# Expert routing taken one attention step earlier, and two shared gating products ahead of the last group's slots

## What is computed

```python
scores = jax.nn.softmax(x2d @ wg_router.T, axis=-1)
topk_w, topk_idx = jax.lax.top_k(scores, TOP_K)
topk_w = topk_w / (jnp.sum(topk_w, axis=-1, keepdims=True) + 1e-20)
pos = jnp.cumsum(oh, axis=0) - 1            
valid = pos_in_e < C
xe = jnp.zeros((E, C, D), x2d.dtype).at[flat_idx, safe_pos].add(x_rep)
...
sh = jax.nn.silu(x2d @ ws_gate) * (x2d @ ws_up) @ ws_down
return y + sh
```

## Time and profile before

| | us |
|---|---|
| median of 3 runs | 635.13 (633.89 to 639.38) |
| the profiled execution's own time | 637.68 |
| its span, first to last instruction | 635.8 |
| DVE busy | 493.5 (78%) |
| PE busy, matmuls | 489.2 (77%) |
| ACT busy | 336.2 (53%) |
| POOL busy | 216.5 (34%) |

### The profile page before, as it was taken

One profiled execution on the slowest core, in us unless ns is written; L12 is line 12 of the kernel. 1 busy time (PEld: TensorE's weight loads), 2 busy tenths in 40 slices (PEclk: granted clock), 3 DMA queues, 4 the chain that ended last, 5 costly groups with the idle time before them and its releaser, 6 DMA issues.

```text
span 635.8 us, 13234 instructions
## 1 busy us (share of the span) xinstructions
PE 489.2 (77%) x4916; PEld 402.2 (63%) x4916; DVE 493.5 (78%) x963; ACT 336.2 (53%) x663; POOL 216.5 (34%) x165
## 2 busy tenths in 40 slices
PE   0268889897725598898959659989999999999930
PEld 0147667675514376676746435589999999999930
DVE  2997999999475789999963680379999999999910
ACT  4334565655565155657532521257777777777720
POOL 3000000000000000000007277508888888888881
PEclk9977999999957699999968988999999999999985
DMA  8999910000000000000002173375997869779323
GB/s 296 282 240 234 249 34 3 1 2 2 2 2 0 0 2 1 3 3 2 1 2 104 31 276 113 125 258 161 244 232 195 227 173 247 203 192 253 37 27 66
DMA packets 56720, 71.89 MB, mean 113 GB/s; under 512 B 11777, under 2 KB 45036, under 8 KB 56544
## 3 DMA queue, kind: packets, MB, share of 16 engines
q1 hardware_dynamic: 40272, 57.35, 31.2%
q0 software_dynamic: 16400, 13.87, 11.0%
HBM read 42.09 MB, written 37.04 MB: 124 GB/s over the span
## 4 chain that ended last, share of the span: by engine, by line
DVE 51%; PE 28%; issue 12%; ACT 5%; DMA 2%; POOL 1%; DVEq 1%; POOLq 0%; SPq 0%; ACTq 0%
DVE negmax L1219 9%; PE S L751 4%; DVE both L1087 3%; DVE wgu_s L1477 3%; DVE fwd L1075 3%; PE S L782 3%; DVE xgT L1496 3%; PE PJ L701 3%; DVE sg L1505 3%; PE S L769 3%; PE S L940 3%; DVE ek L1502 3%; DVE hidden_s L1511 3%; DVE wgu_s L1479 2%; PE S L786 2%
## 5 line engine op out<-in xcount | busy, mean ns | idle before, releaser
L999 PE MATMUL S<-xgT,wgu_s 128*128 128x384 f32 x576 | 108.0, 340 | 8.2 <-DVE sg L1505 7.4
L374 POOL DMA_INDIRECT xe_rows<-x_tok,slot_i x48 | 47.7, 994 | 177.6 <-issue 165.8
L999 PEld LDWEIGHTS S<-xgT,wgu_s 128*128 128x128 f32 x576 | 98.8, 188 | 14.6 <-issue 14.6
L385 POOL DMA_INDIRECT out<-sig,y_token x48 | 81.1, 1690 | 36.9 <-ACT sig L655 22.1
L385 POOL DMA_INDIRECT odd_out<-sig,y_token x48 | 81.0, 1688 | 14.7 <-issue 14.4
L463 ACT ACTIVATE prob<-S 128x1536 f32<-128x1536 f32 x32 | 46.4, 1451 | 60.2 <-PE S L751 59.7
L1219 DVE TENSOR_REDUCE negmax<-S 128x4 f32<-128x512 f32 x64 | 58.2, 952 | 16.2 <-PE S L751 16.2
L782 PE MATMUL S<-q_sb,k_sb 32*128 32x128 f32 (+1 forms) x512 | 37.9, 368 | 29.1 <-DVE negmax L1219 29.1
L365 POOL PARTITION_ALL_REDUCE amax_x<-amax_x x1 | 0.4, 375 | 151.5 <-DVE amax_x L1209 151.5
L782 PEld LDWEIGHTS S<-q_sb,k_sb 32*128 32x128 f32 x512 | 24.6, 196 | 38.6 <-DVE negmax L1219 36.9
L1014 PE MATMUL PJ<-wd_s,hidden_s 128*128 128x256 f32 x320 | 43.3, 282 | 1.9 <-ACT sig L655 1.9
(11 more groups left out here) (212 smaller groups left out, 1083.3 us busy)
## 6 DMA issues: line engine op xcount, KB each, us to landing
xe_rows<-x8m SPq DMA_DIRECT2D x4, 3468.0 KB, 38.7
ratio<-xe_rows SPq DMA_DIRECT2D x32, 433.5 KB, 3.7
ek<-in_wgu SPq DMA_DIRECT2D x32, 384.0 KB, 4.4
x8m<-in_wd SPq DMA_DIRECT2D x32, 256.0 KB, 4.9
x<-in_x SPq DMA_DIRECT2D x1, 1024.0 KB, 7.0
odd_out<-x8m SPq DMA_DIRECT2D x1, 1024.0 KB, 26.5
out<-side SPq DMA_DIRECT2D x8, 128.0 KB, 5.6
out<-odd_out POOLq DMA_DIRECT2D x1, 1024.0 KB, 8.0
```

The lines of the kernel that those rows point to most:

```text
L374: eng.indirect_dma_start(xe_rows, bass.IndirectOffsetOnAxis(slot_i[:, t, k:k + 1], 0), x_tok[:, t, :], None, bounds_check=ROWS - 1, oob_is ...
L385: eng.indirect_dma_start((out, odd_out)[j % 2], bass.IndirectOffsetOnAxis(y_token[:, j, t:t + 1], 0), ye_sb[:, j % 2, t, :], None, bounds_ ...
L999: ins = eng.matmul(S[:, m, 0:CAP], fast(wgu_s[:, j % 2, a, k, m * P:(m + 1) * P]), fast(xgT[:, j % 2, b, k, :]), start=n == 0, stop=n == N ...
```

## The change

- `choose(0)` and `choose(1)` go from the end of steps 11 and 15 to the end of steps 10 and 14; with them ACT's `score_exp` goes from the end to the head of steps 10 and 14.
- `places(0)` and `place_group(0)` go from step 12 to the end of step 11; `places(1)` goes to the end of step 15, ahead of the last `pv`, and `place_group(1)` to the end of DVE's step 15, ahead of the last `scale_o`.
- `places(2)` and `places(3)` go into PE's loop over q, each behind its shared block; `place_group(2)` goes ahead of group 3's `subtract_max`.
- The first two gating products hs go ahead of `place_group(3)`; they were behind it.
- Two waits that guard the PSUM tile TB move by one step with them.

No instruction is added or taken away. The diff (the body of `gate_shared` is the former loop's):

```diff
 ACT, attention
+                        if L and b >= B - 2 and u == 2:
+                            score_exp(b - B + 2)
                         if L and b >= B - 2 and u == 3:
...
-                        if L and b >= B - 2 and u == 2:
-                            score_exp(b - B + 2)
 PE, neg_mm
-                if L and v == QUADS * (B - 1) + 2:
+                if L and v == QUADS * (B - 1) + 1:
                     eng.wait_ge(sem("placing"), 1)
 PE, places
-                    eng.wait_ge(sem("neg_out_1"), min(QUADS * (q + 3) + 2, B * QUADS))
+                    eng.wait_ge(sem("neg_out_1"), min(QUADS * (q + 3) + 1, B * QUADS))
 PE, attention
-                        if L and (b, u) == (B - 1, 0):
-                            places(0)
+                        if L and b >= B - 2 and u == 3:
+                            places(b - B + 2)
                 pv(L, B * QUADS - 1)
-                if L:
-                    places(1)
                 y_mm(L, B - 1)
 PE, behind the attention
                 shared_in(q - EARLY)
-            places(2)
-            places(3)
+                places(q)
             shared_in(2)
 DVE, attention
+                        if L and b >= B - 2 and u == 2:
+                            choose(b - B + 2)
                         if L and b >= B - 2 and u == 3:
-                            choose(b - B + 2)
-                        if L and (b, u) == (B - 1, 0):
-                            place_group(0)
+                            place_group(b - B + 2)
...
                     scale_o(1, B - 1, 1)
-                    place_group(1)
                     residual(1, B - 1)
...
                     choose(2)
+                    place_group(2)
                     subtract_max(3)
                     choose(3)
-                    place_group(2)
+                    gate_shared(0)
+                    gate_shared(1)
                     place_group(3)
 DVE, behind the attention
-            for n in range(TOK // 512 * FST):
...
+            for n in range(2, TOK // 512 * FST):
+                gate_shared(n)
```

More of the change, by code:

```diff
@@ L1371, in place_group, with gate_shared @@
                    .then_inc(sem("slots_made"), 1)
+            def gate_shared(n):
+                rows = slice(0, min(P, FS - n % FST * P))
+                eng.wait_ge(sem("shared_silu"), n + 1)
+                if n >= FST:
+                    eng.wait_ge(sem("base_mm"), 4)
+                eng.tensor_tensor(hs[rows, n % FST, :], sg[rows, n % 2, :], S[rows, n % 2 * 2 + 1, :], ALU.mult)\
+                   .then_inc(sem("shared_h"), 1)
             def attention(L):
```

## The result

The changed kernel took 632.15 us in the median of its first four executions (625.16 to 635.87), the kernel before 636.38 beside it; the ratio is 0.9853 with an interval of 0.9803 to 0.9902. So it is faster by 1.1 to 1.5%, some 7 to 9 us, where 2.6 were forecast. A second profile, of an execution of 628.34 us, stands beside the first.

A forecast was written before the change was run, and what follows sets the result against it. The later of the shared and scatter branches was taken to set the first expert's start and the end. Shared terms -0.4 + 0 - 2.2 + 0 = -2.6 us gave 632.5 us from a median of 635.13, range 627.9 to 636.6.

The forecast's parts named there:

- The two branches: Ahead of the first expert: shared tiles behind the first hs, and POOL's scatters with gathered rows; shared last by 0.48 us.
- Part 1: Steps 10 to 12, choose(0) and place_group(0) earlier: step 13 starts 0.4 us earlier, bounds -2.0 to +3.3.
- I take half clock for step 11, lasting 6.0 to 9.2 us: PE behind its 4.1 us pause ahead of step 11: half clock, so step 12 starts 2.5 to 3.8 us late.
- full, full: Bound with PE at full clock in steps 11 and 12: step 12 starts at 326.6, step 13 gains 2.0 us.
- Part 2: Steps 14 and 15, choose(1) and place_group(1) earlier: group 1's scatters come 4.85 us earlier, 0 on the end.
- on the end nothing: Group 1's earlier scatters gain nothing at the end, unless the branch of the shared tiles gains more than 5 us.
- Part 3: Behind the attention: one place_group leaves the front of the first hs, which comes 2.2 us earlier.
- I take half clock, gain 0: Third shared block on PE: stays at half clock behind a pause of about 3.9 us; gain 0, bounds 0 and 3.3.
- A: Half clock ends in the third shared block: 629.4 us, or 627.8 with steps 11 and 12 full; chance 0.22.
- B: PE keeps full clock in step 11 but loses it in step 12: +0.9 in the attention, 633.8 us; chance 0.18.
- C: Half clock persists through step 12, step 13 starts beyond 337.8: +1.1, 636.2 us, possibly 639; chance 0.12.
- D: The experts' start does not set the end, so time stays 635.1 us; counted within others, chance 0.06.

The follow-up runs named there:

- e2: Kernel before with only the moves behind the attention (places(2), places(3), place_group(2), two gating products earlier); 637.37 us, ratio 1.0032.
- e5: Changed kernel plus one POOL wait that holds group 1's 12 scatters back until y_mm(3); 635.10 us, ratio 1.000.
- e6: Kernel before plus constant products (36 and 64) in PE's two pauses ahead of the third shared block; 639.51 us, ratio 1.0039.
- e10: Kernel before, in its own order, plus constant products in PE's pauses to hold the full clock; 630.55 us, ratio 0.9901.
- e11: Changed kernel with only place_group(2) put back, behind choose(3) and the gating of the first two blocks; 639.03 us, ratio 1.0048.
- slower execution: Changed kernel, no further edit: the first profiled execution, one of three counted as a slower state; 635.69 to 635.97 us.
- faster: Changed kernel, no further edit: the execution of the second profile; 628.34 us.
- e12: Changed kernel with the first two gating products put back behind place_group(3); 631.58 us, ratio 0.9919.
- e9: e8 with more constant products at the boundary of the layers; 623.04 us, ratio 0.9789.
- e4: Changed kernel plus constant products in PE's pauses from step 11 to behind the last projection and ahead of the third shared block; 631.87 us, ratio 0.9932.
- e1: Changed kernel again, no edit, five times beside five of the kernel before; 628.73 us for 635.47, ratio 0.9888.
- e8: Changed kernel plus constant products in all long PE pauses from the end of layer 0's attention on; 625.99 us, ratio 0.9841.
- parts 1 and 2 alone: Kernel before with only choices, places and place_group of groups 0 and 1 a step earlier; 634.44 us, ratio 0.9992.

## Why the prediction was right or wrong

**The two branches: right.** The shared branch and the scatter branch, the 0.48 us between them, the end moving one for one with the first expert (222.35, 222.45 and 222.23 behind it), and the one long wait of POOL's adds: the profiles bear it out. (The issue gaps of the earlier trace rows are 14.8 us, not 14.9.) What the forecast lacked is the far side of a late scatter branch. It counted that only as the later of two ends; e2, e5, e6, e10 and e11 show that the first expert then also runs at half clock, 1.9 to 3.2 us more.

**Part 1: the mechanism right, the size wrong.** The pause ahead of step 11 came at 4.02 us (4.1 forecast), the half clock behind it came, step 12 ran at 1.00 in 7.09 us (7.08), and it was DVE's `place_group(0)` that set its start. The step that failed is "I take half clock for step 11, lasting 6.0 to 9.2 us", and with it "Work of 4.30 takes at most 8.6 then". That work took 7.1 us in the slower execution, the half clock covering 6.1 us of it, and 5.8 in the faster, where it lasted 3.4; in e5, e11 and e12 it is as short as that. So `place_group(0)` on DVE waited little for the places in the slower execution and not at all in the faster one:

```profile
323.40 0.62 DVE L1349 TENSOR_TENSOR x<-x,TB 128x192 f32<-128x192 f32 x2 [0.76 <-PE TB L867]
```

```profile
319.86 0.61 DVE L1349 TENSOR_TENSOR x<-x,TB 128x192 f32<-128x192 f32 x2
```

Counted from the head of step 10, step 12 started 2.1 and 1.2 us later than before, where 2.5 to 3.8 were forecast, and step 13 1.4 and 2.2 us earlier and not 0.4: the faster execution is at the end of the bounds called full, full. And the sum stopped there, at step 13, though the kernel before had a further dip behind it: half clock from 341.2 to 344.6, on the border of steps 13 and 14, where these products take 0.86 us at the full clock:

```profile
342.80 1.51 PE L821 MATMUL OB<-prob,v_sb 128*32 128x256 f32 x16
```

It is absent from the faster execution, and the last projection is 3.23 earlier there and not 2.20.

At the held clock (e9, e10) part 1 is worth 0.1 us the wrong way. By order alone it gains nothing on the attention; it gained only since the kernel before lost 2.3 us there (33.26 for 30.99) behind its pause of 5.48, and the shorter one costs 0.8 (31.90) in the slower execution and nothing (31.06) in the faster. The rule cited from the Trainium skill's page TensorE: Matmul & The Clock Gate, section Part 1: The HAM clock gate, taken alone, asked for half clock in step 12 as well; these traces show 1.00 there, behind 1.10 and 1.52 us of pause. That it covers any pause was the prediction's reading of one sentence, and not what the section says. The same section calls the number of slow products at a start "run-variable", and with that the traces agree: 3.4 and 6.8 us of half clock behind the same pause.

**Part 2: right in size, wrong in its worth.** Group 1's scatters were to come 4.85 earlier and came 4.99 earlier at the same clock (8.3 with what the attention gave). `place_group(2)` was ready in time in the faster execution; in the slower POOL idled 1.90 us for it. But "on the end nothing" was true only under the condition that stands behind it, "unless the shared branch gains more than 5". The shared branch gained 6.7. So without the earlier scatters the whole gain is gone: e5, which takes them away alone, is back at 1.000.

**Part 3: the -2.2 right, the clock not.** Third block 2.10 earlier at the held clock, and 2.20 closer to the last projection in the faster execution; in e12, without the earlier gating, hs is 2.24 later. "I take half clock, gain 0" for the block is the second term that was mis-sized: it took 5.37 us in the faster execution, 1.29 less, and 6.57 in the slower. The pause itself was misjudged: 1.75 or 2.24 us, `places(3)`, then 1.27 or 1.28, not 3.9 with `places(3)` within. In e12, where the second part of it is 3.51, the block takes 6.53.

**The sum.** -2.6 forecast; -6.71 in the faster execution, and the difference is three terms of clock: 1.8 in step 11, 1.0 behind step 13, 1.3 in the third block. In the slower execution the first expert is 2.04 earlier, and that this lies within 0.6 of the forecast is luck: by the last projection 1.06 were gained for 0.4, and behind it 0.9 for 2.2, since half clock around that projection and the first shared block, which the kernel before did not have (1.00 in the earlier trace rows), took back 1.3. It is luck, too, that the median of the first four executions, 632.15, lies next to the 632.5 of the forecast: two are at 625 and 629 and two at 636. The error was to take one clock for both places as the likeliest, and to give the other end 0.22: of the changed kernel's ten executions four lie above 631. More than one per cent faster, which has come (0.9888 and 0.9853), had a chance of 0.11, and no such change 0.86.

**The rivals.** A, with 627.8 to 629.4, is nearest to what happened, and for half of its reason: the clock comes back on both branches, though by three smaller pieces and not by the block's 3.3. The scatters don't cap it: in the faster execution the shared branch is still last, by 1.8 us. B fell: step 12 is at 1.00. C fell: with part 1 in place step 13 stands 31.0 to 31.9 behind the head, in e4 32.9, never beyond the 33.26 of before. Its cousin is real, though: the wait that costs the clock is the one ahead of the first expert, and it makes e11 and e6 slower than before. D fell: the experts' start sets the end, and the same instructions in another order are 6.7 us apart in e1 and, with the clock held, 7.5 in e10 and e9.

What stays open is why half clock behind one and the same pause lasts 3.4 us in one execution and 6.8 in another; no run here sets that. Nor does the length of a pause alone decide whether half clock comes: behind 3.12 us it came (e4, step 12), behind 3.31 it did not (e11, third block):

```profile
373.57 0.19 PE L861 MATMUL OB<-mask_b,tri_b 128*128 128x64 bf16 x1 [3.31 <-DVE y L1349]
...
373.80 3.65 PE L938 MATMUL S<-c_all,ws_gu 128*96 128x512 f32 x8
```

## What to carry to other kernels

Where two branches end within a us of each other, test each part of a change with the other branch in place: here part 3 alone changed the time by +0.3%, parts 1 and 2 alone by nothing that shows (-0.1%, interval -0.4 to +0.3), and all together by -1.1 to -1.5%. Bound every doubtful term of the clock at both ends, carry both to the last row of the sum, and look behind the stretch that was edited, for a dip there may go too. And compare two orders at the same granted clock (constant products in the pauses of both) before saying what the order is worth.

## What was not expected of the hardware

Filling one pause moves the loss to the next one: with products in step 11 the pause of step 12 grew from 1.5 to 3.1 us and its work fell to half clock (e4). The spread of the executions shrank as more were filled: 11 us in the changed kernel (625.0 to 636.0), 6.3 in e4, 3.0 in e8, 1.7 in e9 (622.4 to 624.2). And a wait of PE of 2.9 to 7.4 us for a DMA costs twice: the wait, and 1.9 to 3.2 us by the half clock in the expert behind it (e2, e5, e6, e10, e11), so that e11, whose shared branch is among the earliest, ends later than the kernel before.
